# First attention stage: a position of its own for every call of four parts, six of them changed

## The reference

```python
qkv = layernorm(x) @ w_qkv                          # 32 heads of width 32
attn = softmax(einsum('bhnd,bhmd->bhnm', q, k) * 32 ** -0.5)
out = einsum('bhnm,bhmd->bhnd', attn, v)            # back to rows of 1024
out = out @ w_out + b_out
out = (out - mean(out)) / sqrt(var(out) + 1e-6) * ln_gamma + ln_beta
x = x + out
```

## Time and profile before

| what | us |
|---|---|
| median of three runs | 2883.04 |
| lowest and highest | 2879.36, 2883.94 |
| the profiled execution | 2879.36 |
| its span in the profile | 2877.2 |
| PE, PEld busy | 2605.4 (91%), 1776.4 (62%) |
| DVE, ACT, POOL busy | 2068.8 (72%), 1915.1 (67%), 1671.3 (58%) |
| PE's granted clock, mean | 0.95 of full speed |

### The profile page before, as it was taken

The page is one execution under the profiler, slowest core; times in us unless marked ns, Lnnn a source line. Parts: engine busy times, 40 slices in busy tenths (PEclk is TensorE's granted clock), DMA queues, the critical chain, the costliest instruction groups (busy, mean ns, idle before and its releaser), DMA issues. The chain is left out here.

```text
span 2877.2 us, 51580 instructions
## 1 busy us (share of the span) xinstructions
PE 2605.4 (91%) x18932; PEld 1776.4 (62%) x18932; DVE 2068.8 (72%) x4694; ACT 1915.1 (67%) x4049; POOL 1671.3 (58%) x836
## 2 busy tenths in 40 slices
PE   7999999999999999998997396999999999999286
PEld 6996555555555555546886285566666666665176
DVE  5667888888888889886776543767777777776633
ACT  5665777687777778776775144878778778776133
POOL 0002889797988889893010275656556556554067
PEclk9998999999999999999998597999999999999588
DMA  3014555454545445530001243000000000000133
GB/s 106 1 59 111 127 122 122 113 129 111 137 111 126 118 120 122 125 88 15 20 16 42 68 85 56 2 1 9 9 2 9 9 2 9 9 1 9 39 78 53
DMA packets 144649, 179.21 MB, mean 62 GB/s; under 512 B 30547, under 2 KB 74128, under 8 KB 143888
## 3 DMA queue, kind: packets, MB, share of 16 engines
q1 hardware_dynamic: 130320, 165.20, 22.6%
q0 software_dynamic: 14080, 10.73, 2.7%
HBM read 56.51 MB, written 17.72 MB: 26 GB/s over the span
## 5 line engine op out<-in xcount | busy, mean ns | idle before, releaser
L2047 POOL TENSOR_TENSOR arena<-arena 128x2048 f32<-128x2048 f32 x192 | 881.7, 4594 | 216.6 <-ACT arena L1353 200.3
L1658 DVE TENSOR_REDUCE top<-psum 128x1 f32<-128x512 f32 x1024 | 648.7, 682 | 79.0 <-PE psum L937 79.0
L937 PE MATMUL psum<-stack 98*128 98x512 f32 (+1 forms) x2048 | 606.2, 424 | 14.0 <-ACT arena L1353 9.5
L1353 ACT ACTIVATE arena<-psum 128x512 f32<-128x512 f32 x1024 | 546.8, 600 | 46.5 <-PE psum L937 45.8
L937 PEld LDWEIGHTS psum<-stack 98*128 98x128 f32 (+1 forms) x2048 | 357.7, 191 | 208.9 <-DVE top L1658 85.6
L1008 PE MATMUL psum<-arena,values 128*32 128x512 f32 (+1 forms) x3072 | 482.4, 599 | 3.9 <-ACT arena L1353 2.8
L2057 POOL TENSOR_TENSOR by_query<-by_query,row_tables 128x1024 f32<-128x1024 f32 x170 | 322.0, 1898 | 221.6 <-DVE row_tables L1664 220.9
L1656 DVE TENSOR_REDUCE row_tables<-psum 128x1 f32<-128x512 f32 x512 | 341.1, 679 | 15.9 <-PE psum L945 15.4
L1008 PEld LDWEIGHTS psum<-arena,values 128*32 128x32 f32 (+1 forms) x3072 | 128.6, 119 | 279.1 <-issue 255.6
L1676 DVE COPY arena<-psum 128x512 f32<-128x512 f32 x256 | 174.7, 682 | 138.6 <-PE psum L989 138.5
L2017 POOL TENSOR_SCALAR rstd<-mv 128x4 f32<-128x4 f32 x56 | 13.1, 234 | 415.4 <-DVE mv L1522 413.0
(11 more groups left out here) (208 smaller groups left out, 4710.9 us busy)
## 6 DMA issues: line engine op xcount, KB each, us to landing
stack<-halves SPq DMA_DIRECT2D x768, 128.0 KB, 2.4
qk_ring<-qk_split SPq DMA_DIRECT2D x64, 256.0 KB, 2.9
v_ring<-v_split SPq DMA_DIRECT2D x32, 256.0 KB, 3.0
tokens<-xn SPq DMA_DIRECT2D x16, 256.0 KB, 2.4
arena<-in_wg SPq DMA_DIRECT2D x16, 256.0 KB
arena<-in_wu SPq DMA_DIRECT2D x16, 256.0 KB
arena<-in_wd SPq DMA_DIRECT2D x16, 256.0 KB
wqkv<-in_w_qkv SPq DMA_DIRECT2D x2, 1536.0 KB, 9.1
```

The source lines that it names most:

```text
L937: return T_.matmul(bk, st[0:k, side, h, cols], st[0:k, 1 - side, h, :], start=True, stop=True)
L1353: S_.activation(prob[tile % N_PROB][:, h, :], psum[:, bank[key], :], ACT.Exp, scale=scale).then_inc(released[bank[key]], 1)
L1658: give(V_.reduce_max(top[i][:, j:j + 1], psum[:, bank[key], :], AX.X), key)
L2047: G_.tensor_tensor(to, old, prob[tile % N_PROB], ALU.add).then_inc(summed, 1)
```

## The change

The table WHEN of the first attention is rewritten with lists. For project, maxima and probs the lists hold the former positions, rounded to three places. The mix calls lay at 3.9400, 3.9435, 3.9470 and 3.9505 and now lie at 3.940, 3.944, 3.947 and 3.950; rows stays at 1.950, which for step n + 2 is the place 3.950 of step n. The first two calls of out move from 4.445 and 4.471 to 4.197, the other seven stay where they were, and finish moves from 4.910 to 4.731.

```diff
-    dict(project=(-0.221, 0.718), maxima=(1.027, 1.942), rows=(1.950, 1.950), probs=(2.294, 3.170),
-         last=(3.292, 3.292), mix=(3.940, 3.954), out=(4.445, 4.761), ahead=(-2.284, -0.764),
-         finish=(4.910, 4.910), settle=(5.570, 5.860)),
+    dict(project=[-0.221, 0.092, 0.405],
+         maxima=[1.027, 1.084, 1.141, 1.199, 1.256, 1.313, 1.370, 1.427, 1.484, 1.542, 1.599, 1.656, 1.713, 1.770, 1.828,
+         1.885],
+         rows=(1.950, 1.950),
+         probs=[2.294, 2.346, 2.397, 2.449, 2.500, 2.552, 2.603, 2.655, 2.706, 2.758, 2.809, 2.861, 2.912, 2.964, 3.015,
+         3.067, 3.118],
+         last=(3.292, 3.292), mix=[3.940, 3.944, 3.947, 3.950],
+         out=[4.197, 4.197, 4.498, 4.524, 4.550, 4.577, 4.603, 4.629, 4.656], ahead=(-2.284, -0.764),
+         finish=(4.731, 4.731), settle=(5.570, 5.860)),
```

## The result

The changed kernel is slower: 2915.10 us in the median of four runs (2913.34 to 2922.05) against 2881.40 of the kernel before (2879.36 to 2883.94), a ratio of 1.0124 with a 95% interval of 1.0106 to 1.0141. That is 33.7 us, against 26.7 in the prediction's sum; its time of 2907 was 8 us short; its range was 2889 to 2926. The profiled execution took 2914.81 us with a span of 2912.7.

The account below looks back on a forecast made before the run. PE was taken to bound the first attention. 53 steps x 0.48 = 25.4 us plus 7 x 0.19 = 1.3 made 26.7, giving 2906.1 from the profiled run or 2909.7 from the median, taken as 2907; range 2889 to 2926.

Parts of the forecast that it names:

- k passes from top's bank to dn's and waits for the product with dn.: PE's k in steps 4 to 63: all 60 products load 0.54 us later, 0.48 left per ordinary step.
- DVE executes that product ahead of ml, with 0.12 us more.: DVE, mix: the tie puts the product with dn first; next maximum 0.12 us later, ml done 0.73 later.
- 715.72 + 0.04: DVE: the product with dn starts 0.04 us behind the end of the correction in place, at 715.76.
- 0.06 us are absorbed at the products behind k, nothing further on.: PE, four products behind k: their wait of about 0.06 us goes, leaving 0.48 of the 0.54.
- Project, maxima and probs change nothing; ml's DMA is covered.: Rounded lists swap no neighbours, worth 0; ml's DMA slack falls from 1.35 to 1.10 us, also worth 0.
- Out 0, finish 0.29.: Seven out steps: moving out taken as 0; moving finish lets DVE's next product start 0.29 us earlier.
- The clock as before.: PE's clock: three falls at 1.55 us each in the stage, no change taken, bounds -4.6 to +6.2 us.
- Rival 1: PE's clock falls more often at k's new pauses: 2930 if once in four steps, 3000 if every step; chance 0.08.
- Rival 2: k's wait is absorbed and only DVE's 0.12 us a step counts: 60 x 0.12 = 7, 2890; chance 0.08.
- Rival 3: k waits for nothing: 60 x 0.16 = 10 us less and 2 for finish, 2871; chance 0.04.
- the opening statement that PE loses 0.16 us a step: PE at k in the kernel before: waiting for ml's release was put at 0.16 us lost a step.
- The bounds named for out, finish and the clock: Out -1 to +5 us, finish 0 to 8, clock -4.6 to +6.2; around 26.7 given as 15 to 45.

Follow-up runs that it names:

- the wait moved: Four mix positions alone, plus DVE's wait for the step's output moved to the product before the correction (2913.95 us, ratio 1.0110) or to an earlier maximum (2912.34, 1.0098).
- mix alone: Kernel before with only the four rounded mix positions, out and finish at their old places: 2896.14 us against 2862.96, ratio 1.0120.
- k out of the way: Four rounded mix positions alone, plus k two products later (0.150), against the kernel before: 2889.55 us, ratio 1.0028.
- the kernel with k later: Kernel before with k one product later (0.130 instead of 0.092): 2881.36 us against 2882.07, ratio 0.9997.
- the fastest kernel: Kernel before with the last mix call at 4.088, k one product later (0.130) and finish at 4.731: 2869.60 us against 2883.72, ratio 0.9956.
- bank alone: Kernel before, all positions kept, with dn's bank returned one call earlier in the plan: 2896.95 us, ratio 1.0122.
- order alone: Kernel before with the new mix positions, but dn's bank returned only after top has taken and given its own: 2909.11 us, ratio 1.0166.
- last mix call late: Kernel before with the last mix call at 4.088, behind ml and two maxima: 2883.63 us against 2883.72, ratio 0.9996.

## Why the prediction was right, and what it missed

- *k passes from top's bank to dn's and waits for the product with dn.* Right in all 60 steps. The signs that were named for it are there in kind: L1715 ahead of ml, k's load released by it 60 times and never by ml, the wait behind k gone, L1703 directly behind ACT. In size the steps grew by 0.57 instead of 0.48.
- *DVE executes that product ahead of ml, with 0.12 us more.* The order is right, the size was 0.20. The step that was mis-sized is the start of the moved product, "715.72 + 0.04": it was read off L1700, which has one wait in front of it, while the moved product has two. That is 0.07 us a step, 60 x 0.07 = 4 us, the larger part of what the sum was short of. The experiment with the wait moved elsewhere shows it.
- *0.06 us are absorbed at the products behind k, nothing further on.* Right: 0.62 at k, 0.57 in the step.
- *Project, maxima and probs change nothing; ml's DMA is covered.* Right: ml's waiters at L943 were 5 before and 4 after, although the longest landing of its DMA grew from 2.8 to 3.5 us.
- *Out 0, finish 0.29.* Finish measured 0.27, out -0.11 where its bound was -0.14.
- *The clock as before.* It fell five times instead of three, 3 us, within the bounds given. In the traces the 64 steps grew by 34.6 us, 7.9 over the sum of 26.7; the second wait has 4 of these and the two falls 3. That the falls come from the change is not shown: the kernel with mix alone, with the same pauses at k, has three.
- *Rival 1, the clock swings with the new pauses at k.* False for the change: it fell behind none of the 59 pauses of about 0.5 us, and not behind the first of 1.82. But in the traces of the two kernels with the wait moved it did fall behind the first pause at k, 1.86 and 1.79 us long, so the danger was real for the longest one. Of what the Trainium skill describes in TensorE: Matmul & The Clock Gate, section A second HAM failure mode, no trace here shows a fall behind a pause of 0.5 us.
- *Rival 2, only DVE's delay counts.* False for the change. Yet its chain is real: with k out of the way the loss is 0.19 a step, which is DVE's delay, 0.20 instead of 0.12.
- *Rival 3, 60 x 0.16 = 10 us if k waits for nothing.* Its price was wrong, and with it the opening statement that PE loses 0.16 us a step: the kernel with k later lost that wait and gained 0.00. The wait was real and hid a second chain of nearly the same length. This part of the reading of before was wrong, though the forecast did not rest on it.
- *The range.* The bounds named for out, finish and the clock give 26.7 - 1.0 - 4.6 = 21 at the lower end, not 15, and the forecast's own 2897 to 2922 adds 15 to one base and 45 to another (2882 and 2877). The measured 33.7 lies inside either way.
- *The rule of the Trainium skill that a semaphore between DVE operations costs nothing* (VectorE: DVE Perf Modes, section The DRAIN you can't avoid) was set aside for the rows. The runs bear that out: an operation that waits for a result just made starts 0.03 to 0.04 us behind the end of its predecessor, one without such a wait 0.09 ahead of it, and a second wait in front of the first kind costs 0.07 more.

Not tried: what decides whether a pause of 0.9 us brings the clock down. Such pauses stand in nearly every batch, at the same place, and the same kernel has falls behind some of them; this stays open. So does what holds the fastest kernel at -0.12 instead of -0.22, the sum of both waits; its score products wait 0.25 us for ACT's exponential ahead of k, which may be a third chain.

## What to carry to other kernels

Where an order is sorted by computed times, a tie is a decision: rounding positions by 0.0005 cost 34 us here, because the same order also deals out the banks, and neither the new order on DVE nor the new bank was free by itself. When an order changes, list for each product the last reader of its bank in both versions, not only the neighbours in the queue. And a wait that stands in every step is worth nothing until the chain beside it is measured too: two edits that gave 0.00 and -0.04 a step alone gave -0.12 together.

## What the runs showed of the hardware

A wait on a semaphore that has long been reached is not free in front of an instruction that is itself waiting: 0.07 us on DVE, in both places where it stood in a chain (0.11 against 0.04 behind the predecessor, 0.10 against 0.03 behind ACT). In front of a maximum that has queued work ahead of it, it cost nothing. Where PE waits for the bank of k, its weights load 0.05 us after the end of the DVE operation that frees the bank, whichever it is, in all five arrangements of the order and the bank that ran (before, changed, bank alone, order alone, last mix call late). The clock fell three times in the first 60 steps of before and one to five times in the other kernels' traces, a batch's pause of 0.9 us standing ahead of all but two of these falls; those two stood behind the first pause at k, of 1.86 and 1.79 us (1.82 in the changed kernel, without a fall).
